# Output bias of the GRU layer: four one-row products of TensorE in the output's accumulator, in place of GpSimd's addition to the residual

## What is computed

```python
x = x + _L0_attn_a_ref(_layernorm(x), ...)        # Mamba block: scan with 16 states
x = x + _L0_ffn_ref(_layernorm(x), w_up, w_down)  # ternary FFN, called "a" in the kernel
x = x + _L0_attn_b_ref(_layernorm(x), W1, b1, W2, b2, Wz, bz, Wh, bh, Wo, bo)
x = x + _L0_ffn_ref(_layernorm(x), w_up, w_down)  # the same FFN, called "d" in the kernel

def _L0_attn_b_ref(x, W1, b1, W2, b2, Wz, bz, Wh, bh, Wo, bo):
    x_in = silu(x @ W1 + b1)
    x_skip = silu(x @ W2 + b2)
    h = _min_gru(x_in, Wz, bz, Wh, bh)            # z = sigmoid(..); a scan over the positions
    return (x_skip + h) @ Wo + bo
```

## Time and profile before

| | |
|---|---|
| time, median of 3 runs (lowest, highest) | 849.96 us (849.71, 850.46) |
| the profiled execution's own time | 846.95 us |
| its span | 844.4 us |
| PE busy | 702.1 us, 83% of the span |
| DVE busy | 677.2 us, 80% |
| ACT busy | 641.2 us, 76% |
| POOL busy | 588.8 us, 70% |
| mean granted TensorE clock | 0.921 of full speed |

### The profile page before, as it was taken

How to read it: one execution, slowest core, us unless ns; L and a number is a source line. 1 busy time by engine, 2 the same in 40 slices (tenths; PEclk the granted TensorE clock), 3 DMA queues, 4 the chain that set the end, 5 groups by cost and what they waited for, 6 DMA issues and landing times. The chain is left out here.

```text
span 844.4 us, 12621 instructions
## 1 busy us (share of the span) xinstructions
PE 702.1 (83%) x4116; PEld 593.8 (70%) x4116; DVE 677.2 (80%) x1063; ACT 641.2 (76%) x968; POOL 588.8 (70%) x375
## 2 busy tenths in 40 slices
PE   5655576799788997899789979899799968997995
PEld 5444365588677886688667867688678957786795
DVE  5699988889987998899987998899779988652131
ACT  5787867796889879997899778988898578525403
POOL 4399868777778687878786877968786667515302
PEclk9677776999899999999999999999899989997999
DMA  5511212111112211121111211121111111000000
GB/s 135 180 61 56 73 52 63 52 48 54 38 53 58 68 38 50 40 77 51 50 40 63 63 39 52 43 71 38 50 43 62 49 50 38 1 1 2 13 1 12
DMA packets 35185, 42.79 MB, mean 51 GB/s; under 512 B 7457, under 2 KB 17074, under 8 KB 35122
## 3 DMA queue, kind: packets, MB, share of 16 engines
q1 hardware_dynamic: 35122, 42.00, 16.4%
HBM read 39.63 MB, written 2.36 MB: 50 GB/s over the span
## 5 line engine op out<-in xcount | busy, mean ns | idle before, releaser
L514 POOL TENSOR_TENSOR inflow<-dtu,b_all 128x1024 f32<-128x1024 f32 x127 | 307.9, 2430 | 62.2 <-DVE state L1118 43.8
L1118 DVE TENSOR_TENSOR_SCAN state<-dA,inflow 128x512 f32<-128x512 f32 x256 | 298.2, 1206 | 24.0 <-ACT dA L865 23.7
L865 ACT ACTIVATE dA<-dt,decay_c 128x512 f32<-128x512 f32 x256 | 170.0, 686 | 62.3 <-DVE state L1118 61.2
L1135 DVE TENSOR_TENSOR state<-state,c_ps 128x1024 f32<-128x1024 f32 x128 | 155.4, 1214 | 18.1 <-PE c_ps L1425 13.5
L1434 PE MATMUL y_ps<-ident,state 128*128 128x128 f32 x1024 | 148.1, 293 | 0.0
L1434 PEld LDWEIGHTS y_ps<-ident,state 128*128 128x128 f32 x1024 | 132.4, 152 | 13.2 <-issue 2.7
L1425 PE MATMUL c_ps<-xd,pick 128*128 128x512 f32 x128 | 63.1, 493 | 77.4 <-DVE state L1135 77.1
L1316 PE MATMUL work<-in_hi,wzh_hi 128*128 128x512 f32 x256 | 104.5, 408 | 0.2 <-POOL in_lo L676 0.2
L1317 PE MATMUL work<-in_hi,wzh_lo 128*128 128x512 f32 x256 | 101.0, 395 | 0.0
L1318 PE MATMUL work<-in_lo,wzh_hi 128*128 128x512 f32 x256 | 101.0, 394 | 0.0
L1425 PEld LDWEIGHTS c_ps<-xd,pick 128*128 128x128 f32 x128 | 25.4, 199 | 97.8 <-DVE state L1135 93.3
(11 more groups left out here) (171 smaller groups left out, 1506.2 us busy)
## 6 DMA issues: line engine op xcount, KB each, us to landing
b_all<-b_scratch SPq DMA_DIRECT2D x128, 256.0 KB, 3.1
x_tok<-in_x SPq DMA_DIRECT2D x8, 256.0 KB, 3.8
out_x<-x_tok SPq DMA_DIRECT2D x8, 256.0 KB, 3.6
wide<-in_Wz SPq DMA_DIRECT2D x1, 1024.0 KB, 7.7
wide<-in_Wh SPq DMA_DIRECT2D x1, 1024.0 KB, 8.8
skip_f<-in_W SPq DMA_DIRECT2D x2, 256.0 KB, 4.3
dtu<-in_W_in SPq DMA_DIRECT2D x1, 256.0 KB
mixed<-in_w_up SPq DMA_DIRECT2D x1, 256.0 KB, 2.8
```

Source lines behind the costliest of these rows:

```text
L514: eng.tensor_tensor(inflow[:, n % 2, :, tok(b)], dtu[:, :, tok(b)], b_all[:, n % RING, tok(b)].unsqueeze(1).broadcast_to([P, HALVES, TO[b] ...
L865: act.activation(dA[:, h, tok(b)], dt[:, b % 2, h, tok(b)], ACT.Exp, scale=decay_c[:, h, n:n + 1]).then_inc(s_dA[h], 1)
L1118: dve.tensor_tensor_scan(state[:, g % 3, h, tok(b)], dA[:, h, tok(b)], inflow[:, n % 2, h, tok(b)], first, ALU.mult, ALU.add).then_inc(s_s ...
L1135: dve.tensor_tensor(state[:, g % 3, :, tok(b)], state[:, g % 3, :, tok(b)], c_ps[:, tok(b)].unsqueeze(1).broadcast_to([P, HALVES, TO[b] - ...
```

## The change

The addition on POOL goes, with its semaphore. `bo_tok` is added on PE instead: in front of the first part of `gru_out_skip`, four products, one for each tile, of a row of ones (1 x 128, the stationary operand) with row 0 of `bo_tok` (1 x 128, the moving operand) begin the accumulator. The first skip part no longer begins it, but adds to it.

```diff
-        s_inlo, s_keep, s_hid, s_x2b = (
+        s_inlo, s_keep, s_hid = (
             sem("in_lo_ready"), sem("keep_ready"),
-            sem("hid_ready"), sem("x2b_ready"))
+            sem("hid_ready"))
...
-            def gru_x2b(t):
-                evacuated(pool, t, "a.down")
-                pool.wait_ge(s_ntok[2], t + 1)
-                evacuated(pool, 0, "bo")
-                pool.tensor_tensor(x2_tok[:, tl(t), :], x2_tok[:, tl(t), :],
-                                   bo_tok[:, :].unsqueeze(1).broadcast_to([P, len(tiles(t)), D]), ALU.add).then_inc(s_x2b, 1)
...
-                for t in due(r, s, POOL_ON["x2b"]):
-                    gru_x2b(t)
...
             def gru_x3(t):
                 full(dve, t, "out")
-                dve.wait_ge(s_x2b, t + 1)
                 wait(dve, s_out, 16 * t)
...
             def gru_out_skip(t, k):
                 if k == 0:
                     bank_free(t, "out")
+                    evacuated(pe, 0, "bo")
+                    for j in tiles(t):
+                        pe.matmul(bank("out")[:, cols(j)], ones[0:1, :], bo_tok[0:1, :],
+                                  start=(j == tiles(t)[0]), stop=False, skip_group_check=True)
                 evacuated(pe, t, "in%d" % (FB + k))
                 for j in tiles(t):
-                    pe.matmul(bank("out")[:, cols(j)], skip_f[:, k, cols(j)], wo_sb[:, k, :],
-                              start=(k == 0 and j == tiles(t)[0]), stop=False, skip_group_check=True)
+                    pe.matmul(bank("out")[:, cols(j)], skip_f[:, k, cols(j)], wo_sb[:, k, :], start=False, stop=False,
+                              skip_group_check=True)
```

## The result

The changed kernel took 852.69 us in the median of 9 executions (852.22 to 855.51), the kernel before 849.96 in 9 beside it (846.31 to 851.53): a ratio of 1.0038, 95% interval 1.0024 to 1.0052, or +3.2 us. Measured again beside other kernels, it took 854.50 us in 6 executions (852.65 to 855.08) against 849.67: ratio 1.0058, 1.0040 to 1.0076, or +4.9 us. The ratios are formed from all executions of both kernels and are not the quotients of the medians; for single kernels the two differ by up to 0.16%. So the change makes the kernel about 4 us slower. The forecast was +6.2 us, 856.2.

What follows compares the result with a forecast made beforehand. No engine bounds it alone; Mamba scans set the pace before 728 us, mostly PE after. PE's 1.78 + 0.89 + 0.2 plus 3.36 for the DVE hold made +6.2 on 849.96, 856.2 us; own range 853.5 to 858.5, wider 849.0 to 860.0.

Steps and rivals of the forecast that it cites:

- Units 6 and 7: Output products in the PE-bound tail: the added products lie on the chain, 0.89 us each, 1.78 us together.
- Unit 4: Products delay `a.up0` of unit 5; ACT has no gap until the decay for the scan at 592.78 us: +0.89 us.
- The check that I named: The scan that waits 0.39 us for its decay at 592.78 us should wait over 1 us.
- Unit 2: The C row at 404.43 us comes later than DVE reads it: about +0.2 us from the added products.
- Units 0, 1, 3, 5: PE itself waits for DVE soon after, so the added products cost 0; without that cover, 3.6 us together.
- POOL's 10.2 us: Eight removed POOL additions of 1.27 us each: ACT is just as full there, so they by themselves bring 0.
- The hold: POOL's 2.38 us inflow replaces the addition and holds DVE's L1199 1.12 us longer; units 2, 4, 5 pay, +3.4 us.
- PE alone counts: Rival: what is behind the DVE hold absorbs it, leaving PE's +2.9 us, 852.9 us; chance 0.19.
- Products don't stream: Rival: one-row products cost 3.7 us instead of 0.89 in each unit, 864.5 us in all; chance 0.05.
- POOL as the pace: Rival: steps wait for POOL, so work behind the addition comes 1.27 us earlier in units 1 to 6, 845.3 us; chance 0.12.

Runs made afterwards that it cites:

- pe_add: Kernel before with the four one-row products added in each unit and POOL's addition kept: 853.06 us, ratio 1.0043 to before.
- after_full_pow: Changed kernel with 128-row products, 1e-16 added under the root and POOL's power of -0.5 replacing addition of 1e-8 and reciprocal: 846.41 us, ratio 0.9964 to before.
- before_pow: Kernel before with 1e-16 added under the root and POOL's power of -0.5 replacing addition of 1e-8 and reciprocal: 846.30 us, ratio 0.9969 to before.
- pool_off: Changed kernel without the four new products, so POOL's addition is gone and the output bias left out: 849.51 us, ratio 1.0013 to before.
- pe_full_add: Kernel before with four 128-row products added in each unit and POOL's addition kept: 853.46 us, ratio 1.0042 to before.
- before_again: Kernel before, repeated without an edit for a second profile: 850.08 us, ratio 1.0008 to before.
- pe_tail_add: Kernel before with the four one-row products added in units 6 and 7 alone, POOL's addition kept: 852.75 us, ratio 1.0033 to before.
- before_noeps: Kernel before with FFN d's addition of 1e-8 left out, its reciprocal reading the root straight away: 846.13 us, ratio 0.9977 to before.

## Why the prediction was right in direction and too high in size

**Slower.** It came out slower, inside the range, by 3.2 and 4.9 us for the forecast 6.2. Both mechanisms that the sum was made of are there, and both were mis-sized, in opposite directions, so that the sum came out as near as it did is in part luck. A third term, stretches at the lower clock that come and go with small delays, was not in the sum at all.

**Units 6 and 7, "on the chain, 2 x 0.89 = 1.78 us".** The place is right, the size 2 x 1.28 = 2.56 us. "I take 0.89 us, since the shape of the records is that of L1527" left out the price of the switch between one row and 128. The tail of `pe_add` has +2.39 us. The eight records stand as forecast inside a group; the forecast had no row for its edges.

**Unit 4, "+0.89".** The group moved the scans behind it by 1.27 us in `pe_add` (from -0.04 to +1.23 at 595 us), of which 0.90 came back by 610 us: there DVE waited 2.76 us for `ms_a`, which waits for PE, in the kernel before and only 1.87 us in `pe_add`. Net +0.4. This too is the clock. The kernel before and `pe_add`, in columns as above:

```profile
594.00:609.00 15.00, 11.64 (x69) 10.87 (x70) 11.40 (x15) 11.97 (x20) 11.88 (x8) 0.77 0.13 45
```

```profile
594.00:609.00 15.00, 10.39 (x68) 9.76 (x68) 12.36 (x15) 12.87 (x22) 12.24 (x8) 0.89 0.12 37
```

`after_full_pow` settles it: its clock is 0.77 there as in the kernel before, its group moved the scans by the forecast 0.89 us, and nothing came back (+0.79 in its column from 555 to 645). So the place and the size of this term were right, and the forecast, which followed the delay to the next scan and stopped there, had no term for the clock behind it. The check that I named, a wait of over 1 us before the scan of 592.78 us, came out at 0.65.

**Unit 2, "about +0.2".** +0.44. **Units 0, 1, 3, 5, "I take 0".** Right: no step of `pe_add` at any of them is over 0.3 us.

Together 2.56 + 0.4 + 0.44 = 3.4 us where 2.9 was said, and +3.7 measured.

**POOL's 10.2 us, "by themselves bring 0".** Not contradicted, but not shown. `after_full_pow` against `before_pow` (0.9964 and 0.9969) has the addition gone, nothing held and no difference, but it also has the full-row products, whose own price is 1.78 us in the tail and 0.89 in unit 4. About as much must have come back, by the freed POOL or by the clock (0.920 in the mean of the executions against 0.916). No run has the addition gone, nothing held and no products.

**The hold, "3 x 1.12 = +3.4 us".** The mechanism stood as forecast: 2.33 us in units 1, 2, 4, 5, next to nothing in 3 and 6. In the changed kernel's scans unit 4 lost 0.81 and unit 5 0.80 us where 1.12 was said, and units 1, 3 and 6 nothing. Unit 2 lost 2.3 us at once and 3.1 by 427 us: 1.09 by the hold, as forecast, and 1.25 by the lower clock behind it, which the sum didn't have. What failed besides is the comparison with before: the earlier trace rows are from a profile of 846.95 us, 3.0 us under the median, and I carried that over as a constant shift. It was an execution in which L1060, six microseconds behind `rden_d`, had got through and the clock had stayed up; in the second profile the kernel before loses 2.8 us there. How many of its executions do isn't known. Against the mean of the five profiles with the addition (0, 2.76, 0.44, 2.80 and 0.12, 1.2 us) the hold of unit 2, with what follows it, costs 1.8 us, not 3. Then 0.6 to 2.2 us come back in unit 7, where the profiles with the hold have negative steps from 645 to 733 us and the others 0 to +0.9: in `pool_off` the granted clock is 0.93 from 688 to 713 us, and 0.80 in the same stretch of the first profile of before. The hold's net price is what `pool_off` measured, +1.1 us (-0.3 to +2.5). That unit 7's clock rises because the scans come later is argued, not shown.

**The rival "PE alone counts", 852.9 us,** was nearest in the total, for the reason that it gave: what is behind the hold absorbs much of it. It isn't true that the hold is worth nothing: without it the changed kernel is 2.1 to 3.8 us faster. "Products don't stream" fell (eight records in 1.08 us, not 3.7), as did POOL as the pace.

## What to carry to other kernels

Before an instruction is taken off GpSimd, look at what moves up into its place, and which VectorE instruction starts just behind it: a TENSOR_SCALAR of 128x4 elements took as long as the GpSimd instruction beside it, a RECIPROCAL of the same size didn't, so the cheapest cure is another form of the small instruction. Make the stationary operand of small extra products as tall as its neighbours' when it stands in a stream; it saved 0.39 us a group here, although one of the two pairs of totals (`pe_full_add` against `pe_add`) shows nothing of it. Before a difference between two profiles is put down to an edit, compare the granted clock stretch by stretch. And where a kernel's own executions spread by more than the effect, take two profiles of it first: the one from which all the prices came was one of the lucky ones.

## What the runs showed of the hardware

- A group of eight one-row records in a stream of 128-row products takes 1.28 us, with 128 rows 0.89; the records themselves are alike (270 and 275 ns).
- A DVE TENSOR_SCALAR that starts 0.06 us behind a POOL inflow of 2.37 us lasts 2.33; a RECIPROCAL at the same place lasts 0.18.
- Whether it is held can differ between executions of one kernel: L1060 took 0.16 or 1.33 us. With 1.33 us the scans lost 2.8 us where a stretch at the lower clock followed (`before_again`, `pe_tail_add`), and nothing where none did (`before_noeps`).
- The FFN's last 24 records took 2.7 us in some profiles and 5.1 in others, at 0.90 and 0.69 of the full clock. The tail as a whole follows the products' price plus half of the time at the lower level, within 0.4 us in all of the profiles above.
